# Negated maxima written into the score banks by ScalarE and VectorE, in place of an adding matmul, in the second attention of an audio tower

## The reference

```
qp = (q @ w.T);  kp = (k @ w.T);  vp = (v @ w.T)
scores = einsum('bqd,bkd->bqk', qp, kp) / sqrt(128)
attn = softmax(scores, axis=2)            # over the 7200 keys
out = layernorm((attn @ vp) @ fc.T + fcb + q) * gamma + beta
```

## Time and profile before

| | us |
|---|---|
| median of 3 runs | 1595.29 (1593.91 to 1596.3) |
| the profiled execution | 1597.26 |
| its span, first to last instruction | 1595.4 |
| PE busy | 1506.3 |
| DVE busy | 1062.1 |
| ACT busy | 723.5 |
| POOL busy | 576.5 |

### The profile page before, as it was taken

How to read it: one execution, slowest core, us unless ns; L and a number is a source line. 1 busy time by engine, 2 the same in 40 slices (tenths; PEclk the granted TensorE clock), 3 DMA queues, 4 the chain that set the end, 5 groups by cost and what they waited for, 6 DMA issues and landing times.

```text
span 1595.4 us, 30310 instructions
## 1 busy us (share of the span) xinstructions
PE 1506.3 (94%) x11596; PEld 1014.9 (64%) x11596; DVE 1062.1 (67%) x2085; ACT 723.5 (45%) x1272; POOL 576.5 (36%) x632
## 2 busy tenths in 40 slices
PE   2889998999999799999999999999999999999998
PEld 2456765766666577777777777778885444444444
DVE  5855445565566567677868786855557875876766
ACT  2231122212121255565555565556666665465555
POOL 2220001000110567703370237001995664555655
PEclk9899999999999899999999999999999999999999
DMA  7431110110000368712360325000233442344443
GB/s 209 97 116 30 23 29 22 31 34 21 15 27 27 69 137 171 182 19 62 61 160 6 62 61 130 10 19 2 74 97 103 120 142 89 119 139 126 143 128 109
DMA packets 143773, 128.43 MB, mean 81 GB/s; under 512 B 86837, under 2 KB 124173, under 8 KB 142605
## 3 DMA queue, kind: packets, MB, share of 16 engines
q1 hardware_dynamic: 127053, 110.62, 27.2%
q0 software_dynamic: 2272, 12.06, 2.5%
q10 hardware_dynamic: 14304, 3.81, 1.1%
HBM read 106.21 MB, written 5.28 MB: 70 GB/s over the span
## 4 chain that ended last, share of the span: by engine, by line
PE 80%; DVE 11%; ACT 3%; DMA 3%; POOL 2%; issue 2%; SPq 0%; DVEq 0%; POOLq 0%; ACTq 0%
PE ps L1723 5%; PE ps L1725 5%; PE ps L1724 5%; PE ps L1928 4%; PE ps L2001 4%; PE ps L2002 4%; PE ps L2003 4%; PE ps L1922 4%; PE ps L1923 4%; PE ps L1896 4%; PE ps L1885 4%; PE ps L1891 4%; PE ps L1886 4%; PE ps L1861 3%; PE ps L2013 2%; PE ps L2015 2%
## 5 line engine op out<-in xcount | busy, mean ns | idle before, releaser
L989 ACT ACTIVATE region_c<-ps 128x720 f16<-128x720 f32 (+1 forms) x228 | 175.6, 770 | 258.2 <-PE ps L1896 258.1
L857 POOL TENSOR_TENSOR region_k<-region_c,region_k 128x480 f16<-128x480 f32 x198 | 217.0, 1098 | 170.7 <-ACT region_k L1110 170.6
L1359 DVE TENSOR_TENSOR region_c<-ps,region_c 128x720 f16<-128x720 f32 (+1 forms) x228 | 206.1, 904 | 95.4 <-ACT ps L990 93.1
L1723 PE MATMUL ps<-region_k 128*128 128x360 f16 (+1 forms) x752 | 241.2, 321 | 5.5 <-DVE region_k L1183 4.3
L1725 PE MATMUL ps<-region_k 128*128 128x360 f16 (+1 forms) x752 | 240.8, 320 | 0.0
L1724 PE MATMUL ps<-region_k 128*128 128x360 f16 (+1 forms) x752 | 240.6, 320 | 0.0
L1364 DVE TENSOR_REDUCE region_c<-ps 120x1 f32<-120x512 f32 x252 | 173.6, 689 | 85.9 <-PE ps L1861 83.5
L1922 PE MATMUL ps<-region_k,region_c 128*120 128x129 f16 (+1 forms) x1368 | 180.8, 221 | 0.0
L1923 PE MATMUL ps<-region_k,region_c 128*120 128x128 f16 (+1 forms) x1368 | 180.0, 220 | 0.0
L990 ACT ACTIVATE ps<-ps 128x720 f32<-128x720 f32 (+1 forms) x228 | 174.4, 765 | 0.0
L741 POOL TENSOR_TENSOR vare<-mv,eps 120x6 f32<-120x6 f32 x20 | 4.0, 199 | 464.9 <-DVE mv L1262 464.9
(11 more groups left out here) (277 smaller groups left out, 2821.1 us busy)
## 6 DMA issues: line engine op xcount, KB each, us to landing
gates<-gates_dram SPq DMA_DIRECT2D x384, 120.0 KB, 2.8
region_c<-in_k SPq DMA_DIRECT2D x56, 256.0 KB, 2.9
region_c<-in_v SPq DMA_DIRECT2D x56, 256.0 KB, 3.1
region_c<-in_WcT POOLq DMA_DIRECT2D x8, 1024.0 KB, 7.0
region_c<-in_experts SPq DMA_DIRECT2D x18, 352.0 KB, 3.1
gates<-band_dram SPq DMA_DIRECT2D x26, 189.0 KB
region_c<-in_k POOLq DMA_DIRECT2D x14, 256.0 KB, 3.0
region_k<-region_c SPq DMA_TRANSPOSE x120, 3.1
```

The costliest lines, as they stand in the source:

```text
L857: g.tensor_tensor(a_lo[u], ac[u], a_hi[u], ALU.subtract).then_inc(s["a_lo_ready"], 1)
L1359: v.tensor_tensor(halves(p_lo[u][0:parts]), two(2 * u, parts), halves(p_hi[u][0:parts]), ALU.subtract).then_inc(s["lo_ready"], 1)
L1723: mm(o, wh[:, m, j], xh[:, j:j + w], start=(j == 0), stop=False)
```

## The change

`tower` writes the negated maxima into the score banks before the products, and the products add to them. For half w = 1 ACT does it for tiles 2 to 55, for half w = 0 DVE does it for tiles 4 to 55 (`SEED_BOTH`); the tail and the first tiles keep the adding matmul. For that the negated maxima have to lie on all 128 partitions: at the start of a batch PE makes them in bank 4 with two products of ones and `shift` (`spread_shift` of PE), one after the other, and ACT copies each to `shiftb`, f16 in SBUF (`spread_shift` of ACT), which takes the place of `w2_sb`, no longer needed by then. The maxima of the next batch's tail now come after this. In ACT's list the copy for tile t + 1 stands between the two exponentials of tile t, and it waits for `low_part` of tile t - 1. In DVE's list the copy for tile t + 2 stands directly behind `low_part` of tile t, and waits for it. K(t) is written so that all products of half 0 stand ahead of those of half 1.

```diff
+SEED_BOTH = 4
...
+        shiftb = w2_sb[:].rearrange("p m c -> p (m c)").bitcast(F16)[:, 0:T]
...
+        def act_seeds(b, t):
+
+            return (KT - 2) * b + t - 1
+
+        def dve_seeds(b, t):
+
+            return (KT - SEED_BOTH) * b + t - SEED_BOTH + 1
...
                 a.activation(halves(p_hi[u][0:parts]), st, ACT.Exp).then_inc(s["p_hi_ready"], 1)
+                if t == 0:
+                    spread_shift(b, 1)
+                    spread_shift(b, 0)
+                if 1 <= t < KT - 1:
+                    seed(b, t + 1, 1 - u)
                 a.activation(st, st, ACT.Exp).then_inc(s["exp_sum"], 1)
+
+            def spread_shift(b, w):
+
+                act.wait_ge(s["shift_ps"], 2 * (b + 1) - w)
+                if b:
+
+                    act.wait_ge(s["seed_act"], act_seeds(b, 1))
+                    act.wait_ge(s["seed_dve"], dve_seeds(b, SEED_BOTH - 1))
+                a.activation(shiftb[:, w * HALF:(w + 1) * HALF], bank(4)[:, 0:HALF], ACT.Copy
+                             ).then_inc(s["shift_sb"], 1)
+
+            def seed(b, t, u):
+
+                if t == 2:
+                    act.wait_ge(s["shift_sb"], 2 * b + 1)
+
+                act.wait_ge(s["lo_ready"], TILES * b + t - 1)
+                a.activation(bank(2 * u + 1)[:, 0:HALF], shiftb[:, HALF:T], ACT.Copy).then_inc(s["seed_act"], 1)
...
                 v.tensor_tensor(halves(p_lo[u][0:parts]), two(2 * u, parts), halves(p_hi[u][0:parts]),
                                 ALU.subtract).then_inc(s["lo_ready"], 1)
+                if SEED_BOTH <= t + 2 < KT:
+                    if t + 2 == SEED_BOTH:
+                        dve.wait_ge(s["shift_sb"], 2 * (b + 1))
+
+                    dve.wait_ge(s["lo_ready"], TILES * b + t + 1)
+                    v.tensor_copy(bank(2 * u)[:, 0:HALF], shiftb[:, 0:HALF]).then_inc(s["seed_dve"], 1)
...
+                sh = (shift[b % 2] if b else shift0[:]).rearrange("p r q -> p (r q)")
                 for w in range(2):
                     q = slice(w * HALF, (w + 1) * HALF)
-                    mm(bank(2 * u + w, parts)[:, 0:HALF], kh, q_hi[:, b, q], start=True, stop=False)
-                    mm(bank(2 * u + w, parts)[:, 0:HALF], kh, q_lo[:, b, q], start=False, stop=False)
-                if row is not None:
-                    maximum_of(b + 1, *row)
-                for w in range(2):
-                    q = slice(w * HALF, (w + 1) * HALF)
-                    mm(bank(2 * u + w, parts)[:, 0:HALF], kl, q_hi[:, b, q], start=False, stop=False)
-                if isinstance(t, int) and t == 0:
-                    pe.wait_ge(s["shift_ready"], b + 1)
+                    o = bank(2 * u + w, parts)[:, 0:HALF]
+                    seeded = (2 if w else SEED_BOTH) <= t < KT
+                    if seeded and w:
+                        pe.wait_ge(s["seed_act"], act_seeds(b, t))
+                    elif seeded:
+                        pe.wait_ge(s["seed_dve"], dve_seeds(b, t))
+                    mm(o, kh, q_hi[:, b, q], start=not seeded, stop=False, skip_group_check=True)
+                    mm(o, kh, q_lo[:, b, q], start=False, stop=False, skip_group_check=True)
+                    if w == 0 and row is not None:
+                        maximum_of(b + 1, *row)
+                    last = mm(o, kl, q_hi[:, b, q], start=False, stop=seeded, skip_group_check=True)
+                    if not seeded:
+                        if t == 0:
+                            pe.wait_ge(s["shift_ready"], b + 1)
+                        last = mm(o, ones16[0:P, 0:parts], sh[:, q], start=False, stop=True, skip_group_check=True)
+                last.then_inc(s["st_ps"], 1)
+
+            def spread_shift(b, w):
+
                 sh = (shift[b % 2] if b else shift0[:]).rearrange("p r q -> p (r q)")
-                for w in range(2):
-                    last = mm(bank(2 * u + w, parts)[:, 0:HALF], ones16[0:P, 0:parts],
-                              sh[:, w * HALF:(w + 1) * HALF], start=False, stop=True)
-                last.then_inc(s["st_ps"], 1)
+                mm(bank(4)[:, 0:HALF], ones16[0:P, :], sh[:, w * HALF:(w + 1) * HALF], start=True, stop=True
+                   ).then_inc(s["shift_ps"], 1)
...
-                if b + 1 < B:
-                    prepare_tail(b + 1)
+                spread_shift(b, 1)
...
-                            key_scores(b, 8 * i + t + 1, (t + 1) % 2, row=early)
+                            key_scores(b, 8 * i + t + 1, (t + 1) % 2, row=early if i or t else None)
+                        if i == t == 0:
+
+                            pe.wait_ge(s["shift_sb"], 2 * b + 1)
+                            spread_shift(b, 0)
+                            if b + 1 < B:
+                                pe.wait_ge(s["shift_sb"], 2 * (b + 1))
+                                prepare_tail(b + 1)
+                                maximum_of(b + 1, *first)
```

More of the change, by code:

```diff
@@ L500, in tower @@
             post_full post_free k16_in k16_ready first_ps first_free klo_ready v_split mx_ps mx_free shift_ready
-            st_ps p_hi_ready exp_sum lo_ready pv_done acc_ps acc_free rden_ready wf_done
+            shift_ps shift_sb seed_act seed_dve st_ps p_hi_ready exp_sum lo_ready pv_done acc_ps acc_free rden_ready wf_done
             shifted_logits logits_exp msk_ready gates_ready gate_turned gates_out
```

## The result

The changed kernel takes 1648.54 us (median of 4 runs, 1645.4 to 1652.86) against 1594.6 for the kernel before beside it (4 runs, 1588.49 to 1596.3): 1.0346 times as long, 95% interval 1.0317 to 1.0375. I had forecast 1630 us, slower by 35; it is slower by 54. The profiled execution took 1645.4 us with a span of 1643.6.

The account below looks back on a forecast made before the run. PE issue was taken to bound the second attention, 0.14 us per pair above a chain over bank 4. With 5.62 us per pair, three batches add 33 us and the last 2: forecast 1630 us, range 1600 to 1655.

Parts of the forecast that it names:

- PE bounds now, by 0.14: Second attention before the change: PE needs 5.13 us per pair of tiles, the chain over bank 4 needs 4.99.
- The copies: Added seed copies: ACT's step 0.38 us, length 0.47 to 0.51; DVE's step 0.45, length 0.53.
- The pair: Pair of tiles with maxima after the change: chain over bank 4 takes 5.62 us, against 5.13 before.
- the term 0.04: Chain over bank 4: PE's next maxima product starts 0.04 us after DVE's first reduction ends.
- 85% or less: Sign in the profile after: PE's busy share in the first three batches falls to 85% or less.
- Side steps: Batches with maxima: of 18.8 us side work and batch ends 10.5 stay; 4 us added for DVE.
- The start: Each batch's start: two ACT copies between tile 0's exponentials, the second behind a second PE product, add 1.1 us.
- Batch 3: Last batch, without maxima: chain over the DVE copy takes 4.47 us per pair, the present period; +2 us.
- (a): Whole kernel: PE stays the bound and the seeds are hidden, 64 us fewer, 1532 us; 5% chance.
- (b): Batches with maxima: chain through bank 4 does not close, DVE's load decides, 8 us saved in each, 1573 us; 9%.
- (c): Same chain with copies at their cheap ends and side steps hidden better: 1593 us, no change to tell; 6%.
- (d): PE's idle gaps lower its clock: a tenth of three batches at 1.2 GHz gives 1649 us; 8%.

Follow-up runs that it names:

- e11: Kernel before, both adding matmuls kept, with the second maxima product of a pair issued behind the low-part products: 1591.05 us, ratio 0.999.
- e1: Changed kernel with the DVE copy moved behind the first reduction of the turn in batches with maxima: 1622.24 us, ratio 1.0196.
- e4: Changed kernel with ACT's half (w = 1) only; half w = 0 keeps its adding matmul and DVE copies nothing: 1615.27 us, ratio 1.016.
- e2: Changed kernel with the ACT copy moved behind the in-place exponential: 1640.28 us, ratio 1.0299.
- e3: Changed kernel without both copies and without adding matmuls for the seeded halves, exponential scaled by 0.001 (other output): 1575.12 us, ratio 0.9901.
- e7: Changed kernel with the second maxima product of a pair issued behind the low-part products: 1641.57 us, ratio 1.0307.
- e6: Changed kernel with DVE's half only, its copy behind the first reduction; w = 1 keeps its adding matmul, ACT copies nothing: 1619.34 us, ratio 1.0167.
- e5: Changed kernel with DVE's half only; half w = 1 keeps its adding matmul and ACT copies nothing: 1637.75 us, ratio 1.0279.

## Why the prediction was right in kind and short by 19 us

**PE bounds now, by 0.14.** Right that PE bounds (e11). The margin was smaller: with 0.15 us from the reduction's end to the product, the old chain is 5.10 of 5.13, not 4.99. The old trace could have told: PE waited for the reduction in 7 of its maxima products, and each started 0.14 or 0.15 us after the reduction's end. One of them (timelines of before, DVE and PE):

```profile
775.47 0.69 DVE L1364 TENSOR_REDUCE region_c<-ps 120x1 f32<-120x512 f32 x1
...
776.31 0.40 PE L1861 MATMUL ps<-region_k,region_b 128*120 128x512 f16 x1 [0.29 <-DVE region_c L1364]
```

The reduction ends at 776.16. The prediction took 0.04 with no row for it.

**The copies.** The steps were forecast at 0.38 and 0.45 and are 0.39 and 0.45; the lengths 0.47 to 0.51 and 0.53, and are 0.470 and 0.536. By the Trainium skill, "VectorE: DVE Perf Modes", § Why PSUM operands drop a tier, an operand in PSUM rules out the two-port modes and f32 leaves the basic rate; the trace agrees, as 0.536 us is what the 1.05 ns a column of the PSUM rows gave.

**The pair.** 5.62 forecast, 5.74 measured. The step that failed is the term 0.04 for the release of PE by DVE; it is 0.15. That is 0.11 of the missing 0.12, which makes 3.1 us in 26 pairs. The rows show it, and the expectations for e1 to e4, which had 0.15, came within 0.02 a pair. PE's wait stands where it was put (61 us of 73.6, against "over 40"), 0.81 in the pair above. PE's busy share fell to 87, 85 and 85%, where "85% or less" was the sign.

**Side steps.** I let 8.3 us of 18.8 vanish in PE's new gap and added 4 for DVE: 4.3 to the good. By the table the 26 pairs of batches 1 and 2 gained 26 x 0.61 - 15.0 = 0.9 and 1.1. There this term was too good by 3.4 and 3.2 us. The term that failed is the 8.3: pair by pair 3.6 and 3.2 vanished, while the pairs that DVE or another step makes longer cost 2.8 and 2.1, less than the 4. In batch 0 it came out the other way, 8.1 to the good, so that its total met the forecast (10 for 11) only because two misses cancelled. Why the steps of batches 1 and 2 hide so badly was not settled; the selection steps of the router are a candidate that no run tested.

**The start.** 1.1 us forecast for each batch on top of the longer pair, 1.6 together; measured 1.6 to 2.0 with it, and 3.5 in batch 2. There 1.5 of the 3.5 is a fall of the clock (the last section): where it didn't fall, in e1, e2 and e3, the first pair of batch 2 takes 7.23 in place of 8.75. As e3 has no copies into the banks at all, the start's cost is that of the two shift products and their copies. The timeline of after at the start of batch 2 shows the two shift products and ACT's two copies one behind the other, between its two exponentials of tile 0:

```profile
923.92 0.33 PE L1947 MATMUL ps<-region_c,ones 120*128 120x360 f16 x1
...
924.29 0.47 ACT L1016 ACTIVATE w_sb<-ps 128x360 f16<-128x360 f32 x1 [0.25 <-PE ps L1947]
...
925.32 0.31 PE L1947 MATMUL ps<-region_c,ones 120*128 120x360 f16 x1
...
925.67 0.47 ACT L1016 ACTIVATE w_sb<-ps 128x360 f16<-128x360 f32 x1 [0.91 <-PE ps L1947]
926.03 0.77 ACT L1007 ACTIVATE ps<-ps 128x720 f32<-128x720 f32 x1
```

The in-place exponential starts at 926.03, 2.1 us later than it would, 0.66 behind the first one (which starts at 923.26). I had counted the wait for the first copy but missed that the second product stands behind K(1) in PE's list: 1.03 us pass between the copy's start and that product.

**Batch 3.** Forecast 4.47 a pair and +2; measured 4.57 and +5: the same 0.11 of release once a pair, from DVE's copy to K (the copy ends at 1234.27, K starts at 1234.42), 2.1 us in 26 pairs, and 1.8 at the start.

**Rivals.** (a) did not come: e3 shows that even free seeds give 1575, far from 1532. (b) did not come either: the chain through bank 4 closes as drawn, with PE standing at the product inside the weighing, and e7, which moves that product, shortens the quiet pair. (c) fell with the copies at their middle prices. (d) is refuted as priced: the batches ran at a granted clock of 0.97 to 1.00 with PE idle 0.8 of each 5.7 us. That its 1649 is the measured time is chance. By the rule in the Trainium skill, "TensorE: Matmul & The Clock Gate", § A second HAM failure mode, the clock would have swung throughout; the trace does not agree for the pairs. It shows falls at a batch's start (below) and during the router's logits in the middle of a batch (0.50 from 840 to 845), and the latter the kernel before has too (0.54 from 820 to 825), with PE busy for 5.00 of 5.00 us in both stretches.

**The sum.** Batches +10, +17, +19, +5, against +11, +11, +11 and +2: 51 for 35. The other 3 us can't be placed: the two profiled executions stand only 48 apart, as the one before was 2.7 us above its median and the one after 3.1 below. So the direction, the chain and the place of the wait were right, and three terms were too small: the release, the side steps that stay in batches 1 and 2, and the starts.

## What to carry to other kernels

Where an engine is 98% busy, ask what chain stands next under its period before taking work from it: here 0.61 us of matmuls were taken from a pair in which the chain was 0.03 shorter than the work. A helper's copy costs its full step if it stands ahead of an instruction on that chain, and moving it to the end of its engine's turn puts it on the chain of its own reader, so both places need to be summed. Sum also the pairs with side work and the start of the loop: five quiet pairs in 26 told the right mechanism and too small a price. And a wait that hardly occurs now can still be priced: look for the few places of the old trace in which the engine did stand there.

## What the runs showed of the hardware

How long PE takes to start after the instruction that it stands waiting for went with the number of semaphores that the order list shows ahead of the product. With two it was 0.14 to 0.16 us: the products for the maxima behind DVE's reduction (905.30 to 905.45; 85 rows of the changed kernel, 7 of the one before) and K behind DVE's copy in e6 (890.37 to 890.52; 55 rows). With one it was 0.05 or 0.06: the p_lo products behind DVE's subtraction (19 rows of the changed kernel) and the second half of K behind ACT's copy in e2 (56 rows). So it is not DVE as such that is slow to release PE. No run changed the number of waits alone, so that they are the cause is not shown. DVE behind ACT took 0.03. A row in which the waiting engine is late anyway can't show it.

PE's clock fell at some batch starts and during the router's logits, not in the pairs with their gap of 0.8 us. Busy time in stretches from the start of batch 2, changed kernel (granted clock behind POOL's busy time):

```profile
921.30:925.30 4.00, 3.77 (x23) 1.76 (x22) 1.95 (x10) 2.03 (x5) 3.20 (x7) 1.00 0.00 0
925.30:929.00 3.70, 2.26 (x23) 1.49 (x21) 1.77 (x3) 2.54 (x5) 3.52 (x5) 0.96 0.65 169
929.00:932.70 3.70, 3.70 (x25) 2.53 (x24) 1.83 (x3) 1.10 (x3) 2.62 (x3) 0.57 0.35 66
```

In e7 the same from the start of batch 1:

```profile
734.50:738.50 4.00, 3.06 (x16) 1.13 (x15) 2.67 (x14) 1.54 (x4) 3.20 (x7) 0.83 0.00 0
738.50:742.50 4.00, 3.44 (x16) 1.73 (x14) 0.00 (x0) 1.51 (x3) 1.16 (x1) 0.50 0.66 163
742.50:746.50 4.00, 3.46 (x25) 2.75 (x25) 2.36 (x11) 1.91 (x4) 1.23 (x2) 0.50 0.26 50
```

In e7 PE ran at 1.2 GHz (0.50) for 8 us behind a stretch with 3.06 of 4.00 us busy, and its first pair took 10.8 us. The changed kernel was as busy there (3.06 of 4.00, at 1.00), kept 2.4 GHz, and its first pair took 7.25. Whether it falls at a start differs from trace to trace. That the shift products have a part in it is not shown: e11 has none, and its clock was 0.63 from 726 to 730, at the start of batch 1 (first pair 6.74 against 5.23). The fall costs some 3.5 us in such a batch, also in the first pair of batch 1 of e2 to e5 (10.7 to 11.0). In the profiled executions of e2, e3, e5 and e7 it is part of why the times came out above what the pairs promised.
